# Deformable convolutions: offsets clamped to a step by VectorE instead of a distance by ScalarE, and spreads issued in threes

## What is computed

```python
def _bilinear_sample(x, py, px):
    y0 = jnp.floor(py); x0 = jnp.floor(px)
    for dy in (0.0, 1.0):
        for dx in (0.0, 1.0):
            yi = y0 + dy; xi = x0 + dx
            wy = 1.0 - jnp.abs(py - yi)
            wx = 1.0 - jnp.abs(px - xi)
            ...
            out = out + v * (wy * wx * valid.astype(x.dtype))[None]

def _block(x, dc_w, dc_b, of_w, of_b, dw, db):
    h = jax.nn.relu(_deconv2d(x, dc_w, dc_b))
    offset = _conv2d(h, of_w, of_b, PAD)
    return jax.nn.relu(_deform_conv2d(h, offset, dw, db))
```

## Time and profile before

| | |
|---|---|
| median of 3 runs | 4314.02 us (4310.0, 4314.37, 4314.02) |
| span of the profiled execution | 4314.1 us |
| TensorE busy | 3880.1 us, 90% |
| VectorE busy | 2952.5 us, 68% |
| ScalarE busy | 2786.4 us, 65% |
| GpSimd busy | 1140.5 us, 26% |
| mean granted TensorE clock | 0.940 |

### The profile page before, as it was taken

One profiled execution on the slowest core, in us unless ns is written; L12 is line 12 of the kernel. 1 busy time (PEld: TensorE's weight loads), 2 busy tenths in 40 slices (PEclk: granted clock), 3 DMA queues, 4 the chain that ended last, 5 costly groups with the idle time before them and its releaser, 6 DMA issues.

```text
span 4314.1 us, 221726 instructions
## 1 busy us (share of the span) xinstructions
PE 3880.1 (90%) x81908; PEld 2973.5 (69%) x81908; DVE 2952.5 (68%) x5858; ACT 2786.4 (65%) x6651; POOL 1140.5 (26%) x645
## 2 busy tenths in 40 slices
PE   4998799699789879979988997998799999799998
PEld 3776577477567657756765775776577777577776
DVE  5885687488567668847856884784577774577775
ACT  2885588388478658837865883885355554255554
POOL 0441243134033214403322431331111110111111
PEclk8999899799989989989998997999799999899999
DMA  4442544344244334424424443443766664666664
GB/s 125 127 127 66 143 125 110 89 126 127 75 132 126 90 106 127 125 76 131 126 71 127 127 114 92 126 125 109 179 154 152 150 150 127 147 154 152 152 150 110
DMA packets 244838, 533.50 MB, mean 124 GB/s; under 512 B 61200, under 2 KB 151824, under 8 KB 227216
## 3 DMA queue, kind: packets, MB, share of 16 engines
q1 hardware_dynamic: 194224, 498.67, 45.0%
q10 hardware_dynamic: 50240, 29.89, 2.4%
HBM read 471.87 MB, written 56.45 MB: 122 GB/s over the span
## 4 chain that ended last, share of the span: by engine, by line
PE 68%; SPq 18%; issue 7%; ACT 2%; DMA 2%; DVE 2%; POOLq 0%; ACTq 0%; DVEq 0%; POOL 0%; PEld 0%; PEldq 0%
PE P L544 26%; PE PS L562 24%; SPq L380 9%; PE P L515 8%; PE PS L575 8%; SPq L388 8%; SPq L370 1%; PE PS L515 1%; ACT H L848 1%; DMA X<-x_dram 1%; PE P L530 1%; DVE FOFF L1032 1%; DMA VT<-ht_store 0%; DVE A L917 0%; DVE ST L1036 0%
## 5 line engine op out<-in xcount | busy, mean ns | idle before, releaser
L917 DVE TENSOR_TENSOR A<-P,YC 121x384 f32<-121x384 f32 (+1 forms) x4608 | 2311.4, 550 | 850.1 <-ACT YC L768 684.5
L544 PE MATMUL P<-HL,SEL 32*121 32x384 f16 (+1 forms) x21504 | 1745.6, 304 | 131.6 <-issue 95.3
L768 ACT ACTIVATE YC<-P 121x384 f32<-121x384 f32 (+1 forms) x4608 | 1733.9, 444 | 98.7 <-PE P L544 65.8
L544 PEld LDWEIGHTS P<-HL,SEL 32*121 32x121 f16 (+1 forms) x21504 | 1126.9, 117 | 513.9 <-issue 228.6
L562 PE MATMUL PS<-A,VT 121*32 121x80 f32 (+1 forms) x40960 | 1342.7, 250 | 51.7 <-DMA VT<-ht_store 15.5
L562 PEld LDWEIGHTS PS<-A,VT 121*32 121x32 f32 (+1 forms) x40960 | 1093.0, 117 | 354.6 <-issue 200.4
L1103 POOL CAST HL<-DIST 128x1152 f16<-128x1152 f32 x320 | 366.3, 1145 | 3066.1 <-DVE DIST L922 3043.8
L745 ACT ACTIVATE SMP<-PS 128x480 f32<-128x480 f32 (+3 forms) x1152 | 593.9, 516 | 638.2 <-PE PS L562 632.9
L1105 POOL TENSOR_TENSOR HL<-DIST,HL 128x1152 f16<-128x1152 f32 x320 | 769.6, 2405 | 58.5 <-POOL HL L1103 58.5
L735 ACT ACTIVATE DIST<-HB,CONST 128x1152 f32<-128x1152 f32 x320 | 400.8, 1252 | 231.4 <-DMA HB<-off_store 128.8
L575 PE MATMUL PS<-SMP,CW 128*64 128x128 f32 x7424 | 476.0, 277 | 5.4 <-ACT SMP L745 5.4
(11 more groups left out here) (61 smaller groups left out, 703.4 us busy)
## 6 DMA issues: line engine op xcount, KB each, us to landing
HB<-off_store SPq DMA_DIRECT2D x2560, 72.0 KB
VT<-ht_store SPq DMA_DIRECT2D x256, 512.0 KB
VT<-ht_store SPq DMA_DIRECT2D x768, 132.0 KB
VT<-ht_store SPq DMA_DIRECT2D x256, 88.0 KB
off_store<-FOFF SPq DMA_DIRECT2D x160, 128.0 KB, 2.6
H<-x_dram SPq DMA_DIRECT2D x5, 2048.0 KB, 14.6
ht_store<-A ACTq DMA_DIRECT2D x32, 256.0 KB, 3.3
ht_store<-VT ACTq DMA_DIRECT2D x32, 256.0 KB, 3.9
```

What stands on the lines that cost most here:

```text
L544: mm = nc.tensor.matmul(dst, SEL[q, table, 0:sh.npos], hats, start=part == 0, stop=part == 1)
L768: nc.scalar.activation(YC[0:sh.npos, g % X_SLOTS, 0:sh.size], P[0:sh.npos, g % Y_SLOTS, 0:sh.size], ACT.Copy).then_inc(y_ready, 1)
L917: return nc.vector.tensor_tensor(dst, x, y, ALU.mult)
```

## The change

Four things change.
- **The distance pass is gone.** VectorE clamps `HB` directly between two bounds that differ by row (`STEP_FROM`, `STEP_TO`, one column of `CONST` each) and so makes `DIST` in one instruction, a step that rises from the bound below to the bound above. `abs_done` is gone: `HB` is released by `clamp_done`. VectorE itself now waits for the load of `HB` and, inside the loop, for `hats_full`.
- **The hat is a difference of steps.** The tables in `SEL` hold +1 at a position and -1 at the next, so that the spread yields the hat less one. The constant is put back after it: ACT's copy becomes Identity with a scale and a bias read per row (`ONE`), and the product becomes a scalar_tensor_tensor, `(x + SCALE) * y`. Making `SEL` takes two more small instructions a step.
- **Spreads go in runs in kind 0 too** (`run`): y of up to three groups, then x of the same.
- **Group 11 is carried over**, where no part is sampled after it: PE spreads it at the head of the next chunk's (in kind 1 the next batch's) first run, with groups 0 and 1. The other engines keep their order.

```diff
@@ Shape
+        self.carries = int(self.ngr - 1 not in self.after)
@@ sync
-                    sp.wait_ge(abs_done, c - 1)
+                    sp.wait_ge(clamp_done, c - 1)
                     load_offsets(band, half)
@@ tensor
+                def run(members):
+                    if len(members) > Y_SLOTS:
+                        run(members[:Y_SLOTS])
+                        members = members[Y_SLOTS:]
+                    for n, g, b, half in members:
+                        pe.wait_ge(y_ready, n + 1)
                         spread(sh, g, b, half, y_table, g % Y_SLOTS).then_inc(y_full, 1)
+                    for n, g, b, half in members:
+                        pe.wait_ge(product_done, n + 1)
                         for tile, table in enumerate(x_tables):
                             mm = spread(sh, g, b, half, table, Y_SLOTS + g % X_SLOTS, sh.size * tile)
                         mm.then_inc(x_full, 1)
...
+                    for g in range(sh.ngr - sh.carries):
+                        if g in sh.runs:
+                            members = [(first + each, each, b, half) for each in sh.runs[g]]
+                            if sh.runs[g][0] == 0 and sh.carries and carried is not None:
+                                members.insert(0, (first - 1, sh.ngr - 1, *carried))
+                            run(members)
@@ scalar
-                wait_alone(act, hb_full[half], 32 * IMG * (band + 1))
-                nc.scalar.activation(DIST[:, :], HB[:, half, :], ACT.Abs, bias=HAT_BIAS).then_inc(abs_done, 1)
...
-                            if sh.kind == 0 and g == sh.next_at and not last:
-                                next_distance(c + 1, band + half, 1 - half)
...
-                                                 ACT.Copy).then_inc(y_ready, 1)
+                                                 ACT.Identity, bias=ONE[0:sh.npos], scale=1.0 / SCALE ** 2).then_inc(y_ready, 1)
@@ vector
-                return nc.vector.tensor_tensor(dst, x, y, ALU.mult)
+                return nc.vector.scalar_tensor_tensor(dst, x, SCALE, y, ALU.add, ALU.mult)
-            def clamp(c):
-                dve.wait_ge(abs_done, c + 1)
-                nc.vector.tensor_scalar(DIST[:, :], DIST[:, :], SCALE, SCALE, ALU.min, ALU.subtract).then_inc(clamp_done, 1)
+            def clamp(c, band, half):
+                if not isinstance(c, int):
+                    dve.wait_ge(hats_full, c)
+                wait_alone(dve, hb_full[half], 32 * IMG * (band + 1))
+                nc.vector.tensor_scalar(DIST[:, :], HB[:, half, :], STEP_FROM, STEP_TO, ALU.max, ALU.min).then_inc(clamp_done, 1)
```

More of the change, by code:

```diff
@@ L610, in spread_x, with batch @@
                         mm.then_inc(x_full, 1)
[L612 to L621, removed]
+                def batch(c, b, half, prev, before, carried):
+                    first = (c * sh.batches + b) * sh.ngr
+                    for g in range(sh.ngr - sh.carries):
[4 more added lines that the diff above has]
+                            run(members)
                         if prev is not None:
@@ L633, in body @@
                             prev = (c, band, b - 1, half)
+                            carried = (b - 1, half)
                         elif before == 0:
-                            prev = None
+                            prev = carried = None
                         else:
                             prev = (c - 1, band + half - 1, sh.batches - 1, 1 - half)
-                        batch(c, b, half, prev, before)
+                            carried = (sh.batches - 1, 1 - half)
+                        batch(c, b, half, prev, before, carried)
                 def tail():
+                    if sh.carries:
+                        run([(CHUNKS * sh.batches * sh.ngr - 1, sh.ngr - 1, sh.batches - 1, 1)])
                     if sh.lag == 2:
@@ L952, in body @@
                             if b == 0 and g == sh.next_at + 1 and not last:
-                                clamp(c + 1)
+                                clamp(c + 1, band + half, 1 - half)
                             if before >= sh.lag and b == sh.batches - 1 and g == sh.sum_after + 2:
@@ L1058, in step @@
                 flag_count[0] += 1
-                clamp(0)
+                clamp(0, 0, 0)
                 chained()
@@ L1137, in _tables @@
         for n in range(16 * columns):
-            sel[:, 2 + tile, first + n] = is_x & (q == j + LANES * (n % columns))
-            sel[:, 4, first + n] = ~is_x & (q == n // columns)
+            for of, table, mine in ((j + LANES * (n % columns), tile, is_x), (n // columns, 2, ~is_x)):
+                after = 1.0 * (mine & (q == of + 1)) if of + 1 < AXIS else 1.0 * (MARGIN - AXIS + 1) / MARGIN * (mine & (q == 0))
+                sel[:, 2 + table, first + n] = 1.0 * (mine & (q == of)) - after
+                sel[:, 5 + table, first + n] = (mine & (q == of)) / SCALE
     pxc = np.zeros((STRIPES, CH, STRIPE_ROWS, COLS), np.float32)
```

50 lines of the change are left out of this document (22 added, 28 removed).

## The result

The changed kernel takes 4325.22 us (median of 20 runs, 4318.76 to 4334.31) against 4312.98 of the kernel before beside it (20 runs): ratio **1.0029, 95% interval 1.0023 to 1.0036**. Its profiled execution has a span of 4322.0 us, 7.9 more than before's 4314.1. The sign was wrong. The medians lie 12.2 us apart; what follows splits the 7.9 of the two profiled executions.

A forecast was written before the change was run, and what follows sets the result against it. It took PE and SP's DMA queue, side by side, to bound layers 1 to 4, and PE the last layer. 4314.1 less 4 x 3.97 and 5.8 gave 4293 us, range 4275 to 4330.

The forecast's parts named there:

- The sum: Whole kernel: 4314.1 less four gains of 3.97 us and less 5.8 us in the last layer, giving 4293 us.
- nothing from the last layer and 3 us less from the others: Whole kernel: the case behind the forecast's upper bound, given as 4305 us.
- The bound: Layers 1 to 4: PE and SP's queue run side by side; the queue issues for 8.55 us a chunk.
- 4 x 3.97 = 15.9: First group's four samplings in layers 1 to 4: each can gain 3.97 us on SP's queue, no more.
- The order of threes: TensorE, layers 1 to 4: spreads in runs of three save little off the bound; costed at nothing, covered by SP's queue.
- -0.17 a chunk by the carry: Last layer: groups 11, 0 and 1 run together ahead of the sums, 0.63 us instead of 0.80.
- Where PE waits for copy, then product, then x spread: +0.08: Last layer, groups 11 to 4 without samples between: the dearer copy adds 0.08 us once a chunk.
- 0.75 again, 0.9 at worst: VectorE's clamp: with per-row operands it keeps its pace, 0.75 us, at worst 0.9, and VectorE's total stays under 8.55.
- Rival 5: TensorE's clock falls because PE idles about a microsecond in each chunk: +380 us, 4700 us; chance 0.03.
- Rival 2: Last layer: four runs a chunk each wait for the previous run's last copy, +10 us, 4308 us; chance 0.14.
- The copy: ScalarE's copy: the per-row bias adds 0.08 us, and the pitch goes from 0.39 to 0.47 us.
- the full-price rival: ScalarE: copies cost +0.23 us, a pitch of 0.62, and become the bound at 9.2 us a chunk, 4480 us; chance 0.14.

The follow-up runs named there:

- e13: Kernel before, with four of a chunk's eight offset loads issued by GpSimd instead of SP: 4335.02 us, ratio 1.0058.
- e14: Changed kernel, with four of a chunk's eight offset loads issued by GpSimd instead of SP: 4236.18 us, ratio 0.9825.
- e4: Kernel before, with only the new order of TensorE's spreads (runs of up to three, group 11 carried over): 4332.73 us, ratio 1.0043.
- e17: Changed kernel, with the copy's constant as an immediate and four of eight offset loads issued by GpSimd: 4135.77 us, ratio 0.9585.
- e3: Changed kernel, with group 11 no longer carried into the next run: 4334.71 us, ratio 1.0044.
- e2: Kernel before, with its ScalarE copies adding a per-row operand, a column of zeros: 4388.30 us, ratio 1.0167.
- e7: Kernel before, with its clamp reading two per-row operands of the same numbers instead of two immediates: 4342.17 us, ratio 1.0070.
- e1: Changed kernel, with the copy's constant as an immediate instead of a per-row operand: 4302.24 us, ratio 0.9970.
- e8: e1 with layers 1 to 4 in the old order of spreads (single images, no carry there): 4293.78 us, ratio 0.9951.
- e11: e8 with four of a chunk's eight offset loads issued by GpSimd instead of SP: 4110.22 us, ratio 0.9527.
- e9: e8 with the last layer's clamp moved to where VectorE idles during TensorE's sums: 4337.59 us, ratio 1.0060.
- e15: e9 with the last layer's residual also moved, from group 3 to group 10 of the second batch: 4294.04 us, ratio 0.9959.
- e5: Kernel before, with a chunk's eight offset loads issued as four merged ones of the same bytes: 5794.88 us, ratio 1.3432.
- e6: e1 with a chunk's eight offset loads issued as four merged ones of the same bytes: 5801.61 us, ratio 1.3447.

## Why the prediction was wrong, step by step

- **The sum.** Predicted was -15.9 - 5.8 = -21.7 us, the profiles have +7.9. The 29.6 between them are 5.2 too much gain in layers 1 to 4, some 14 in the undisturbed chunks of the last layer (+8 for -5.8), and some 10 of dropped clock. The upper bound was also added up wrongly: "nothing from the last layer and 3 us less from the others" gives 4314.1 - 12.9 = 4301, not 4305.
- **The bound.** "PE and SP run side by side and either looks like the bound" was right, and the numbers were 8.59 (PE's chain, whole in mid-sampling) and 8.55 (queue). That the queue then caps the gain was right: window spacing 17.09, chunks of 8.55, slack used up to 7.31. e13 and e14 show it: against the kernel before, the changed kernel is 99 us faster when both have the shorter queue, and 12 slower with the long one.
- **4 x 3.97 = 15.9** came out as 10.7. In the first sampling, the one that was read, the slack was taken (11.23 to 7.31 = 3.92), but the two free chunks behind it take 7.97 and 7.50, where they took 7.68 and 7.11 before: 0.7 given back at the end of each such sampling, so some 13; where the rest went is open. The order of threes, costed "at nothing", is that under the queue and nowhere else: e4 and e17 show 0.14 and 0.12 us a chunk lost, not gained.
- **The last layer, where the sign was lost.** "-0.17 a chunk by the carry": measured exactly so (e4 -0.17, e3 +0.17). "Where PE waits for copy, then product, then x spread: +0.08": the operand costs +0.16 (e2). "0.75 again, 0.9 at worst", and no price on the path, for the clamp: 871 ns, +0.13 a chunk (e7). Together -0.17 + 0.16 + 0.13 = +0.12, as the profile shows (+0.13), 8 us instead of -5.8. These two terms are the step that failed. My ruler for the clamp was an instruction of 4096 columns with another operation, 0.59 ns each, and I read from it that the pace is kept. It holds a fixed part too: both it (2414 ns) and the new clamp (871 ns) read two per-row operands, and the difference, 1543 ns for 2944 columns, is 0.52 ns a column, which leaves some 267 ns. At that pace the old clamp (751 ns) leaves 147. By this estimate the two operands cost 120 ns an instruction and nothing per column. The bound of 0.9 was known, but I let it touch no path because VectorE's sum stayed under the chunk; a sum says nothing of the place.
- **The clock.** Rival 5 asked about it for layers 1 to 4, where from 900 to 1020 us it stayed at 1.00. It fell where I had not looked: in the last layer, after a copy and a product made TensorE wait at the edge of a chunk, some 10 us in all (18.6 - 8; the seven drops counted make 9.1). e1 and e2 tie it to the operand: away with the immediate, there with the operand alone. With the immediate TensorE waits more in layers 1 to 4 and the clock does fall there at times, to 0.98 on average in e1's third sampling, where the chunk stays the queue's all the same:

```profile
860.00:1085.00 225.00, 203.36 (x5180) 152.44 (x5176) 190.01 (x371) 174.25 (x422) 94.64 (x54) 0.98 0.45 127
```

- **Rival 2**, the last layer paying more than once for the operand, had the right place and sign: +10 against the 18.6 found; its mechanism, one price per run, gave 4 x 0.08, and e2 has 0.16, two such prices; the rest of its distance is the clamp and the clock, which it did not have.
- **The copy.** +0.08 a copy was +0.09, the pitch of 0.47 exact; the full-price rival (0.62) fell. The Trainium skill (ScalarE: Activation LUTs, What ACT_TABLE_LOAD costs) puts 93 ns on a pointer operand; the runs have 592 - 500 = 92 and 424 - 333 = 91, and agree.
- **The product** and **SP** at nothing: right (552 against 549; same spacing).

## What to carry to other kernels

When two bounds lie within 1% of each other, price a change against both, and ask what the second one gives before the first is shortened: here 2% (the changed kernel to e14) and 4.3% (e8 to e11) lay behind four DMA issues in a queue for which the kernel before did not wait in mid-sampling. A constant that is the same in all rows belongs in an immediate. An engine's total under the chunk's length does not make a longer instruction free; look at what stands behind it in its queue, and at what another engine does meanwhile.

## What the runs showed that I had not expected

- A scalar_tensor_tensor of 128 columns with both inputs in SBUF, begun just behind GpSimd's tensor_tensor, waits it out: 2.48 us instead of 0.34 (e9). Three products, which read one input from PSUM, begin during the same instruction and take 1.49 us, as they do elsewhere (e15).
- Half as many offset loads for the same bytes held the queue twice as long, and the whole took a third longer (e5, e6).
- GpSimd, busy for 26% of the span in the kernel before, issues an offset load in 494 ns (SP: 3.85 / 8 = 0.48 us).
- The granted clock drops for some 3 us behind a chunk's edge with waits of 0.16 and 0.15 us and thinly placed spreads, in seven chunks of the last layer and not in others with much the same edge; what tells them apart stays open.
